# Transposes of the feed-forward input as DMAs of SyncE, another order of filler work in attention pass 6, two banks for the gates

## The reference, cut to what matters

```python
# per sequence: T = 4096 tokens, D = 1024, 16 heads of 64, causal; hidden width 3072
Q, K, V = proj(Wq), proj(Wk), proj(Wv)
O = softmax(scale * Q @ K.T, causal) @ V
x = layernorm(x + O @ Wo.T)
gate = x @ wg.T; up = x @ wu.T              # wg, wu, wd: int weights / 127
h = silu(gate) * up
x = layernorm(x + h @ wd.T)
```

## Time and profile before

| | us |
|---|---|
| median of 3 runs | 1301.59 |
| runs | 1461.5, 1300.77, 1301.59 |
| the profiled execution, device time | 1303.55 |
| its span (slowest core, 7) | 1302.5 |
| spans of the 8 cores | 1296.7 to 1302.5 |
| PE / ACT / DVE / POOL busy | 1249.0 / 705.1 / 451.9 / 182.7 |

### The profile page before, as it was taken

How to read it: one execution, slowest core, us unless ns; L and a number is a source line. 1 busy time by engine, 2 the same in 40 slices (tenths; PEclk the granted TensorE clock), 3 DMA queues, 4 the chain that set the end, 5 groups by cost and what they waited for, 6 DMA issues and landing times.

```text
span 1302.5 us, 26270 instructions; the slowest of 8 cores (1296.7 to 1302.5 us)
## 1 busy us (share of the span) xinstructions
PE 1249.0 (96%) x9974; PEld 677.4 (52%) x9974; DVE 451.9 (35%) x813; ACT 705.1 (54%) x794; POOL 182.7 (14%) x258
## 2 busy tenths in 40 slices
PE   4989999999999999999988999999999999999997
PEld 2645656656656566665554544444444444444443
DVE  1444344343543434423344575212221322132123
ACT  0058878888788898889979755111112211301123
POOL 2001111122021120212223011210011011101100
PEclk9989999999999999999999999999999999999999
DMA  9932323224232232232745023850245134504512
GB/s 139 164 67 50 58 50 59 42 58 75 43 67 42 50 67 42 50 59 50 147 114 155 9 74 115 292 159 17 81 149 157 67 113 146 167 27 134 157 50 113
DMA packets 39448, 119.84 MB, mean 92 GB/s; under 512 B 13344, under 2 KB 13344, under 8 KB 37152
## 3 DMA queue, kind: packets, MB, share of 16 engines
q0 software_dynamic: 24672, 100.68, 32.7%
q1 hardware_dynamic: 14656, 17.47, 4.2%
HBM read 145.13 MB, written 27.39 MB: 132 GB/s over the span
## 4 chain that ended last, share of the span: by engine, by line
PE 86%; ACT 5%; another core or an unknown queue 5%; issue 2%; DVE 1%; DMA 1%; POOL 0%; SPq 0%; DVEq 0%; ACTq 0%
PE pp L357 20%; PE ops L714 16%; PE dps L1175 13%; PE gps L1121 13%; PE ups L1115 13%; PE sps L660 9%; ACT pt L670 5%; PE dps L1020 2%; DMA ident<-identd 1%; PE tps L1046 0%; DVE vbuf L400 0%; DVE pt L690 0%; ACT x1T L1052 0%; PE pp L432 0%
## 5 line engine op out<-in xcount | busy, mean ns | idle before, releaser
L670 ACT ACTIVATE pt<-sps,cbias 128x1024 bf16<-128x1024 f32 x544 | 569.9, 1116 | 89.9 <-PE sps L660 84.5
L714 PE MATMUL ops<-pt,vbuf 64*65 64x512 bf16 (+3 forms) x2560 | 328.6, 344 | 7.2 <-DVE pt L690 3.7
L1127 ACT ACTIVATE sgb<-gps 128x512 bf16<-128x512 f32 x96 | 57.3, 597 | 369.6 <-PE gps L1121 369.6
L660 PE MATMUL sps<-qbuf,kbuf 64*128 64x512 bf16 (+3 forms) x1280 | 220.5, 346 | 8.3 <-ACT pt L670 7.0
L714 PEld LDWEIGHTS ops<-pt,vbuf 64*65 64x65 bf16 x2560 | 152.9, 107 | 87.9 <-issue 25.6
L357 PE MATMUL pp<-xb,wkq 64*128 64x512 bf16 x1344 | 190.9, 380 | 2.3 <-DVE cbias L472 1.0
L1115 PE MATMUL ups<-x1T,wgu 128*128 128x512 bf16 x768 | 181.4, 379 | 0.0
L1121 PE MATMUL gps<-x1T,wgu 128*128 128x512 bf16 x768 | 181.4, 379 | 0.0
L1175 PE MATMUL dps<-wd,hbuf 128*128 128x512 bf16 x768 | 166.4, 379 | 0.0
L1130 DVE SCALAR_TENSOR_TENSOR hbuf<-ups,sgb 128x512 bf16<-128x512 f32 x96 | 66.4, 692 | 260.7 <-ACT sgb L1127 260.7
L756 POOL TENSOR_TENSOR ofm<-ostg,lb 64x512 bf16<-64x512 f32 x64 | 82.2, 1285 | 369.9 <-DMA lb<-linvd 367.5
(11 more groups left out here) (71 smaller groups left out, 606.0 us busy)
## 6 DMA issues: line engine op xcount, KB each, us to landing
wgu<-wgub POOLq DMA_DIRECT2D x96, 512.0 KB, 3.8
wgub<-wguP POOLq DMA_DIRECT2D x24, 512.0 KB, 6.0
xb<-xP POOLq DMA_DIRECT2D x8, 1024.0 KB, 36.0
lb<-linvd SPq DMA_DIRECT2D x32, 256.0 KB, 3.6
x<-xtok POOLq DMA_DIRECT2D x16, 512.0 KB, 7.5
yout<-x SPq DMA_DIRECT2D x15, 512.0 KB, 2.7
wdb<-wdP POOLq DMA_DIRECT2D x12, 512.0 KB, 6.0
wd<-wdb POOLq DMA_DIRECT2D x6, 1024.0 KB, 8.0
```

Source lines behind the costliest of these rows:

```text
L660: mm = pe.matmul(buf[:, h * 512 + so:h * 512 + so + w], kt[r, kb * 128:kb * 128 + 128], qt[r, g * 512 + q0:g * 512 + q0 + w], start=True, ...
L670: exp_at[j] = s_act.inc(act.activation(pt[j % NPT][:, :], buf[:, :], AF.Exp, bias=cbias[(p + s["late"]) % 2][:, 0:1]))
L714: mm = pe.matmul(ops[:, h * 512 + q0:h * 512 + q0 + w], vt[r, c0:c0 + 65], pt[j % NPT][r, h * 512 + so:h * 512 + so + w], start=(s["first" ...
L1127: gps_free[0] = s_act.inc(act.activation(sgb[j][:, :], gps[:, :], AF.Silu, scale=QS))
```

## The change

1. A semaphore `s_tr` for each of the three `ybf` buffers is new. `turn(t, ready)` issues 8 DMA transposes of 128x128 bf16 from `ybf` into `x1T` on SyncE's queue. It takes the place of TensorE's transposes and of the copies out of PSUM, for all 16 tiles. For early tiles it is put into the order six steps after the tile's moments. Whoever writes `ybf` again waits for the DMAs of three tiles earlier. `gate_up(g)` waits for the DMAs of its four tiles.
2. PSUM: `tps` is gone, and `gps` has two banks.
3. `LIGHT` for pass 6 is (0, 2, 7, 14) in place of eighteen entries.
4. Where `firsts` had one wait for the latest exponential or mask of its steps, `values` now waits for its own step.

```diff
@@ values @@
             if half_turn == 0:
+                wait(pe, pt_at[j][0], pt_at[j][1])
                 if s["first"]:
@@ ybf_early @@
-            wait(dve, s_pe, ybf_free[t % 3])
+            wait(dve, s_tr[t % 3], ybf_free[t % 3])
@@ early_half @@
                     pending.append((tick[0] + 5, lambda: ybf_early(t)))
+
+                    pending.append((tick[0] + 6, lambda n=s_pe.n: turn(t, n)))
@@ in place of early_turn @@
-        def early_turn(t):
+        def turn(t, ready):
+
             g, k = t // 4, t % 4
...
+            wait(sp_q, ybf_at[t][0], ybf_at[t][1])
+            wait(sp_q, s_pe, ready)
             for c in range(NCH):
...
+                s_tr[t % 3].inc(sp_q.dma_start_transpose(
+                    x1T[g][:, c * 512 + k * 128:c * 512 + k * 128 + 128],
+                    ybf[t % 3][:, c * 128:(c + 1) * 128]), 16)
+            ybf_free[t % 3] = s_tr[t % 3].n
+            x1T_at.setdefault(g, []).append((s_tr[t % 3], s_tr[t % 3].n))
@@ table @@
-                 (0, 2, 5, 6, 7, 9, 10, 11, 12, 13, 16, 17, 18, 19, 20, 21, 22, 23),
+                 (0, 2, 7, 14),
@@ firsts @@
-                for sem in (s_act, s_dve):
-                    got = [pt_at[j][1] for j in steps if pt_at[j][0] is sem]
-                    if got:
-                        wait(pe, sem, max(got))
@@ normalised @@
-            wait(act, s_pe, ybf_free[t % 3])
+            wait(act, s_tr[t % 3], ybf_free[t % 3])
@@ after attention @@
             out_proj(t)
-            while turned[0] <= t - 2:
-                turn(turned[0])
-                turned[0] += 1
...
+            turn(t, att_pe)
@@ gate_up @@
-            wait(pe, x1T_at[g][0], x1T_at[g][1])
+            for sem, value in x1T_at[g]:
+                wait(pe, sem, value)
...
-                wait(pe, s_act, gps_free[0])
+                wait(pe, s_act, gps_free[j])
@@ main loop @@
             gate_up(g)
-            while turned[0] < NTT:
-
-                turn(turned[0])
-                turned[0] += 1
             down(g)
```

More of the change, by code:

```diff
@@ L205, in build_program @@
         s_cv = Sem(st, nc, "s_cv")
+        s_tr = [Sem(st, nc, f"s_tr{i}") for i in range(3)]
         dve.memset(onesb[:, :], 1.0)
@@ L781, in build_program @@
         early_next = [0]
-        turned = [0]
         over = [False]
@@ L850, in early_tiles @@
                 yield from early_half(t, 1)
-                while turned[0] <= t - 2 and not over[0]:
-                    if turned[0] in ybf_at:
-                        turned[0] += 1
-                        yield from early_turn(turned[0] - 1)
-                    else:
-                        yield WAITS
             yield from turn_on(None)
@@ L986, in build_program @@
         att_act = exp_at[NJ - 1]
-        att_dve = s_dve.n
         att_ps.close()
@@ L993, in build_program @@
         ups = [st.enter_context(nc.psum_tensor(f"ups{i}", [128, 512], F32)) for i in range(2)]
-        gps = st.enter_context(nc.psum_tensor("gps", [128, 512], F32))
-        tps = st.enter_context(nc.psum_tensor("tps", [128, 1024], BF16))
+        gps = [st.enter_context(nc.psum_tensor(f"gps{i}", [128, 512], F32)) for i in range(2)]
         dps_free = [[(s_act, att_act)] * 2, [(s_act, att_act)] * 2]
-        tps_free = [(s_dve, att_dve)]
         def rstd_shift(t, ready):
@@ L1039, in normalised @@
             ybf_at[t] = (s_act, n)
-        def turn(t):
-            g, k = t // 4, t % 4
-            wait(pe, ybf_at[t][0], ybf_at[t][1])
-            wait(pe, tps_free[0][0], tps_free[0][1])
-            for c in range(NCH):
-                mm = pe.transpose(tps[:, c * 128:(c + 1) * 128],
-                                  ybf[t % 3][:, c * 128:(c + 1) * 128], ident[:, :])
-            ybf_free[t % 3] = s_pe.inc(mm)
-            wait(act, s_pe, s_pe.n)
-            dst = x1T[g][:, :].rearrange("p (c q) -> p c q", c=NCH)[:, :, k * 128:(k + 1) * 128]
-            src = tps[:, :].rearrange("p (c q) -> p c q", c=NCH)
-            x1T_at[g] = (s_act, s_act.inc(act.copy(dst, src)))
-            tps_free[0] = (s_act, s_act.n)
         wgu_free = [att_pe] * NWB
@@ L1093, in build_program @@
                 ybf_early(t)
+            turn(t, att_pe)
         wo_done = s_pe.n
         wait(pool, s_pe, wo_done)
-        gps_free = [0]
+        gps_free = [0, 0]
         ups_free = [0, 0]
@@ L1118, in gate_up @@
                 s_pe.inc(mm)
-                wait(pe, s_act, gps_free[0])
+                wait(pe, s_act, gps_free[j])
                 for c in range(NCH):
-                    mm = pe.matmul(gps[:, :], wgu[i][:, c * 128:(c + 1) * 128],
+                    mm = pe.matmul(gps[j][:, :], wgu[i][:, c * 128:(c + 1) * 128],
                                    xt[:, c * 512:(c + 1) * 512],
@@ L1126, in gate_up @@
                 wait(act, s_dve, sgb_free[j])
-                gps_free[0] = s_act.inc(act.activation(sgb[j][:, :], gps[:, :], AF.Silu, scale=QS))
+                gps_free[j] = s_act.inc(act.activation(sgb[j][:, :], gps[j][:, :], AF.Silu, scale=QS))
                 wait(dve, s_pe, max(wgu_free[i], h_free[0]))
```

## The result

| | before | after |
|---|---|---|
| median, us | 1301.18 (4 runs, 1299.8 to 1461.5) | 1365.32 (4 runs, 1362.23 to 1366.94) |
| ratio of the times | | 1.0488, 95% interval 1.0475 to 1.0501 |
| span of the profiled execution | 1302.5 | 1364.1 |

A forecast was written before the change was run, and what follows sets the result against it. ScalarE and PE were taken to share the bound in attention, PE alone after it. From 1301.6, 11.9 gained (10.0 transposes, 1.9 table) and 3.1 stall lost gave 1292.8, said as 1293; 8-in-10 range 1284 to 1335.

The forecast's parts named there:

- the ring of three buffers: Three `ybf` buffers tie tile 15 to turn 12, so VectorE's first gate product waits for 56 DMAs behind the last broadcast.
- the forecast's own formula: PE's stall in `gate_up(0)` before its first product: 56c - 24.9 us where positive, 3.1 us at c = 0.5.
- The back-up in pass 7: Beyond c = 0.92 turns queue up in pass 7; at c = 1.3 turn 4 ends at 766, delaying the chain 15 us.
- The dear rival: SyncE's queue becomes the bound: at c = 1.3 stall 63 us, time 1353; slower by over 2% had chance 0.20.
- slowed weight loads: Sign of being wrong: transposes that slow the weight loads of the gates; no size given.
- the wait for `ofm` at tile 12: Sign of being wrong: PE waits at `out_proj` tile 12 for the last unit's `ofm`; no size given.
- Transposes off PE: `out_proj` tiles 3.6 us, last gate to `down(0)` 2.4, last exponential to tile 8 4.0: together 10.0 us gained.
- The table: New order in pass 6, effects in passes 6 and 7: net 1.9 us gained, bounds 0.9 and 9.7.
- The forced filler: End of pass 6: ScalarE idled 1.85, 3.86 and 2.79 us for bias chain and filler; 8.5 us gained by removing it.
- the whole turns of pass 6: Seven more three-step periods with a whole turn cost 7 x 0.7 = 4.9 us, two of two steps 1.5: 6.4 lost.
- The rival that the table gives nothing: Pass 6: added whole turns cost what forced filler did, waits cost 3, time 1298; inside the 1290 to 1302 case, 0.42.
- Waits and banks at 0: Two gate banks gain nothing; a wait for each first half in attention taken as 0, bounds 3.7 us gained or lost.

The follow-up runs named there:

- the table in between: Kernel before with `LIGHT` for pass 6 as (0, 2, 7, 14, 19 to 23): 1298.41 us; the changed kernel with it and one DMA a tile: 1290.27 us.
- the earlier reciprocal: Last unit's reciprocal of row sums moved three steps ahead, against the kernel with one DMA a tile and the table in between: 1286.14 us, ratio 0.9887.
- the third staging buffer: Kernel before with the new table for pass 6, plus a third `ostg` buffer for the output of unit 29: 1307.61 us, ratio 1.0022.

## Why the prediction was wrong

**The failed step is the size of c,** the time for which one transposing DMA holds SyncE's queue. The mechanism, the ring of three buffers, the two in-order engines and the 56 DMAs between the last broadcast and tile 12's landing, is what happened. I took c = 0.5 us from plain DMAs of 0.33 to 0.49 and gave 0.20 to a dear one. Measured are 1.23 us of hold and (851.33 - 780.04) / 56 = 1.27 with the gaps, where 851.33 is the moment at which the last of them left the queue; it landed 2.41 later. With it the forecast's own formula gives 56 x 1.27 - 24.9 = 46.2; the wait is 46.24. That this agrees to a tenth is partly luck: the formula lets the broadcast leave at 763.5 and TensorE run out of gates at 793.1, and both came some 16 us later, at 779.9 and 809.1. The back-up in pass 7 was set at 15 us for c = 1.3, with turn 4 ending at 766, and it ended at 766.8; the broadcast is 19.3 us later against the last exponential than before, and TensorE reaches the gates 9.2 later than before where 7.6 earlier (4.0 and 3.6) was forecast, so 17 us. The dear rival's 63 us, which it put into one stall, came as 46 in the gates and 17 ahead of them, and that rival, not the forecast, was the right case. No row of before told 0.5 from 1.3. What was wrong was to take the plain DMA as the nearest row although it was known that a transposing one does another thing, and to let a range end at 1335 while c = 1.3 gave 1353.

**The remaining 12 us** between the rival's 1353 and 1365 are smaller terms. The matmuls after the stall ran at 1.2 GHz, +1.8. Weight loads came 6.9 us late on the slowest core (0 to 1.5 us on the other seven): GpSimd's loads had stood behind the gates for the whole stall, and came when transposes were still in flight. I had named slowed weight loads as something that would prove me wrong, like the wait for `ofm` at tile 12 (6.73 us here), and had given them no price. And the table lost where I had a gain; in the changed kernel pass 7 took 80.83 us at a granted clock of 0.96. With 1.9 + 3.4 for it these make 14 us; they were measured in different kernels, and their sum is only about the 12 that are missing.

**Transposes off PE: right in place, a little large.** Forecast 10.0 us. The kernel with one DMA a tile against the one with the same table and waits but transposes on TensorE: 1295.7 - 1304.0 = -8.3. With the table in between: 1290.3 - 1298.4 = -8.1. The wait for `ofm` at tile 12, 3.6 to 4.8 us where at most 0.2 stood before, covers the missing 2 us; the earlier reciprocal brought it down to 1.6 to 2.6 us and the time by 4.1.

**The table: wrong by 5 us.** Forecast 1.9 gained, measured 1.0026 x 1301.6 - 1301.6 = 3.4 lost. The forced filler went, all but 1.1 us of the 8.5; the other terms that failed are the whole turns of pass 6 (some 0.8 for 0.7 each, so that the pass did not get shorter where 2 us were forecast) and pass 7, where I counted work and not what stands behind a quicker one: three small DMAs in a row, a buffer that waits for them, and the clock that falls there. The rival that the table gives nothing had the sign but not this cause.

**Waits and banks at 0: right**, 0.9996 and +1.5 us within the intervals.

**Transposing against plain DMAs.** The Trainium skill, "Advanced Engine Details and Errata", X-Bar Transpose (TRN2), says that transpose DMAs are as fast as regular ones. For the landing the trace agrees: 2.4 us for 32 KB and 3.1 for 256 KB, beside 2.8 and 3.6 of the plain ones of 4 and 256 KB in the earlier trace rows. For what the issuing queue pays it does not, 1.23 against 0.33 to 0.53 us; one instruction of 256 KB pays the same 1.23, where the plain broadcast of 256 KB pays 0.45. The lower rating of the hardware path on the same page (DGE: Hardware vs Software) pointed the right way, without a number.

## What to carry to other kernels

Ask of a DMA that an in-order queue issues not how long it takes to land but how long it holds the queue, and how many stand between two things that somebody waits for; if the hold is one per instruction, make the instruction larger before anything else. If no row of the profile shows the operation, the case in which it is dear gets its full width in the range. And where a stretch is made quicker, look up which chain of small transfers it will now catch up with, since the wait can cost more than its length when the clock falls with it.

## What the runs showed of the hardware that was not expected

- A transposing DMA holds SyncE's queue for 1.22 to 1.23 us (medians) whether it carries one 128x128 block, two or eight; it lands 2.4 us after its issue with one block or two, 3.1 with eight.
- The same 4 KB DMA out of SBUF, 2.8 us in the median, landed in 8.1 us on one core and 12.1 on another of one execution; its chain of three was 5.2 us later there, and TensorE waited 4.1 us longer.
- In pass 7 under the new table TensorE ran for 3.4 or 6.8 us at 1.2 GHz near idle times of 0.7 to 5.8 us, and with the third staging buffer three such falls came with no idle time over 0.7 us close ahead (on cores 0, 1 and 2, at 666.1, 685.1 and 667.4 us).
- With eight transposes a tile in flight beside the weight loads of the gates TensorE waited 13.0 us in all for weights on one core and 0.5 on another of the same execution; with the transposes on TensorE it waited on none.
